# First group's loads reordered in a LoRA + dense kernel: identity behind W's first halves, W's blocks ahead of x, the adapters' rows spread over more steps, the small product one tile later

## The reference, cut to what matters

```python
x = x + (x @ B0[id0].T) @ A0[id0].T            # rank 16, scaling 1
x = x + x @ W.T + b + 2.0 * (x @ As[id1]) @ Bs[id1]   # W 2048 x 2048, rank 16
```

## Time and profile before

| | us |
|---|---|
| median of 3 runs | 1398.6 |
| lowest and highest of them | 1396.78, 1398.95 |
| the profiled execution's own time | 1398.88 |
| its span, first to last instruction | 1396.9 |
| PE busy in the span | 1372.8 |
| DVE busy | 943.6 |
| ACT busy | 529.1 |
| POOL busy | 79.1 |
| bytes moved by DMA | 311.60 MB, mean 223 GB/s |
| granted TensorE clock, mean | 0.997 |

### The profile page before, as it was taken

One profiled execution on the slowest core, in us unless ns is written; L12 is line 12 of the kernel. 1 busy time (PEld: TensorE's weight loads), 2 busy tenths in 40 slices (PEclk: granted clock), 3 DMA queues, 4 the chain that ended last, 5 costly groups with the idle time before them and its releaser, 6 DMA issues.

```text
span 1396.9 us, 16200 instructions
## 1 busy us (share of the span) xinstructions
PE 1372.8 (98%) x6024; PEld 1128.8 (81%) x6024; DVE 943.6 (68%) x1049; ACT 529.1 (38%) x588; POOL 79.1 (6%) x163
## 2 busy tenths in 40 slices
PE   6899999999999999999999999999999999999999
PEld 5788877888888878888888888888888888888887
DVE  4677897777877887687765566665755566665662
ACT  3444444433334443343324453333233444333321
POOL 2012010001010000001001000000101000000000
PEclk9999999999999999999999999999999999999999
DMA  9789764778888987599895335455856343555642
GB/s 343 242 293 306 264 238 147 243 236 282 297 292 307 314 297 264 178 301 327 287 358 194 110 112 180 163 175 168 276 204 189 117 135 134 169 167 189 194 151 83
DMA packets 98591, 311.60 MB, mean 223 GB/s; under 512 B 13009, under 2 KB 14289, under 8 KB 98513
## 3 DMA queue, kind: packets, MB, share of 16 engines
q1 hardware_dynamic: 92736, 298.96, 63.1%
q0 software_dynamic: 5776, 11.61, 2.9%
HBM read 254.94 MB, written 55.57 MB: 222 GB/s over the span
## 4 chain that ended last, share of the span: by engine, by line
PE 91%; DVE 4%; DMA 2%; issue 1%; ACT 1%; SPq 1%; ACTq 0%; DVEq 0%
PE acc L590 27%; PE acc L591 27%; PE acc L592 27%; DMA w_two<-w 2%; PE acc L565 2%; PE down_ps L549 2%; PE down_ps L550 2%; PE image_ps L535 1%; PE image_ps L529 1%; PE image_ps L530 1%; DVE w_one L759 1%; DVE bg_lo L794 1%; DVE w_lo L767 1%; DVE x_lo L789 0%; ACT w_hi L627 0%
## 5 line engine op out<-in xcount | busy, mean ns | idle before, releaser
L590 PE MATMUL acc<-x_hi,w_hi 128*128 128x512 f32 x1792 | 702.1, 392 | 16.3 <-DVE x_lo L789 12.5
L591 PE MATMUL acc<-x_lo,w_hi 128*128 128x512 f32 x1792 | 699.5, 390 | 0.0
L592 PE MATMUL acc<-x_hi,w_lo 128*128 128x512 f32 x1792 | 699.1, 390 | 0.0
L627 ACT ACTIVATE w_hi<-w_one 128x1024 fp32r<-128x1024 f32 x223 | 235.9, 1058 | 541.1 <-PE acc L592 504.5
L767 DVE TENSOR_TENSOR w_lo<-w_one,w_hi 128x1024 fp32r<-128x1024 f32 x223 | 273.1, 1225 | 215.2 <-ACT w_hi L627 215.2
L590 PEld LDWEIGHTS acc<-x_hi,w_hi 128*128 128x128 f32 x1792 | 337.6, 188 | 89.0 <-issue 16.6
L591 PEld LDWEIGHTS acc<-x_lo,w_hi 128*128 128x128 f32 x1792 | 337.6, 188 | 71.7 <-issue 1.0
L592 PEld LDWEIGHTS acc<-x_hi,w_lo 128*128 128x128 f32 x1792 | 337.3, 188 | 71.2
L660 ACT ACTIVATE sums<-acc 128x512 f32<-128x512 f32 x96 | 57.1, 594 | 203.7 <-PE acc L592 188.1
L826 DVE SCALAR_TENSOR_TENSOR sums<-acc,bias_sb,sums 128x512 f32<-128x512 f32 x128 | 95.7, 747 | 22.0 <-PE acc L565 20.8
L759 DVE TENSOR_TENSOR w_one<-w_one,w_two 128x1024 f32<-128x1024 f32 x79 | 96.4, 1220 | 17.1 <-DMA w_two<-w 17.1
(11 more groups left out here) (61 smaller groups left out, 610.3 us busy)
## 6 DMA issues: line engine op xcount, KB each, us to landing
w_one<-w SPq DMA_DIRECT2D x143, 512.0 KB, 5.5
w_one<-w_sums SPq DMA_DIRECT2D x80, 512.0 KB, 3.7
w_two<-w SPq DMA_DIRECT2D x79, 512.0 KB, 7.4
x_stage<-x SPq DMA_DIRECT2D x64, 512.0 KB, 4.4
out<-sums SPq DMA_DIRECT2D x128, 256.0 KB, 4.6
w_sums<-w_one SPq DMA_DIRECT2D x40, 512.0 KB, 4.1
resident<-x SPq DMA_DIRECT2D x32, 512.0 KB, 8.6
bg_raw<-w_rows SPq DMA_DIRECT2D x32, 512.0 KB, 5.0
```

The lines of the kernel that those rows point to most:

```text
L590: pe.matmul(ps[:, :], w_hi[ws][:, c, :], hi, start=(c == 0), stop=False)
L591: pe.matmul(ps[:, :], w_hi[ws][:, c, :], lo, start=False, stop=False)
L592: mm = pe.matmul(ps[:, :], w_lo[ws][:, c, :], hi, start=False, stop=(c == H - 1))
L627: act.activation(w_hi[s % W_PARTS][:, :, :], w_one[s % W_ONES][:, :, :], ACT.Copy).then_inc(w_hi_ready, 1)
```

## The change

It touches only the first group. SP loads the identity as its third transfer (behind the first halves of W's first two blocks) into a corner of `sums`, and ACT copies it into `identity_sb`; POOL no longer loads it. SP loads chunk 0 of batch 0's x ahead of the loop and chunks 1, 2, 3 at steps 0, 2, 3 (behind that step's W loads); A1's eight loads go to steps 1, 2, 3 as 2, 3, 3. POOL's eight A0 loads wait until `w_two` of step 1 has landed. The splits of A0's rows move from the loops' step 2 to step 3, A1's copy from step 3 to step 4 and behind split_bg, the small product behind step 5, its mask to step 6. Sums and splits of x for product 1 are at (1, 3, 6, 7) and (5, 6, 7, 7). The image chunks in steps 4 to 16 are distributed 1, 2, 3, 2, 3, 3, 2, 3, 3, 2, 3, 3, 2. `across` is multiplied ahead of chunk 7, 6, 6, 4 of its eight.

```diff
--- before.py
+++ after.py
@@ -52,15 +52,26 @@
 X_SPLIT_AT = (2, 4, 7, 7)
+A_RESIDENT_AT = {0: 1, 2: 2, 3: 3}
+A1_LOAD_AT = ((1, (0, 1)), (2, (2, 3, 4)), (3, (5, 6, 7)))
 def split_at(p):
-    return X_SPLIT_AT if p > 1 else (4, 5, 7, 7)
+    return X_SPLIT_AT if p > 1 else (5, 6, 7, 7)
+def sum_at(p):
+    return X_SUM_AT if p > 1 else (1, 3, 6, 7)
 IMAGE = 32
+ACROSS_AT = (7, 6, 6, 4)
 def where(s):
@@ -82,7 +93,7 @@
         places = (0, 2, 4, 6)
         return [IMAGE + 16 * g + 4 * i + places.index(o)] if i < 4 and o in places else []
     if 4 <= s <= 16:
-        counts = (2, 3, 2, 3, 2, 3, 2, 3, 2, 3, 2, 3, 2)
+        counts = (1, 2, 3, 2, 3, 3, 2, 3, 3, 2, 3, 3, 2)
         first = sum(counts[:s - 4])
         return list(range(first, first + counts[s - 4]))
     if 19 <= s <= 22:
@@ -246,6 +257,7 @@
         mask_sb = sums[1][:, 0, 0:P]
+        identity_raw = sums[0][:, 0, 0:P]
         across = sums[1][:, H - 1, T - P:T]
         a1_cols = sums[1][:, CH - 1:H - 1, :].rearrange("p o t -> p (o t)")
@@ -260,6 +272,7 @@
         mask_loaded = sem("mask_loaded")
         b1_rows_loaded = sem("b1_rows_loaded")
         identity_loaded = sem("identity_loaded")
+        identity_ready = sem("identity_ready")
         a1_ready = sem("a1_ready")
         across_done = sem("across_done")
         across_ready = sem("across_ready")
@@ -408,13 +421,14 @@
                 for tile, (k, q) in zip((w_one[0], w_two[0]), W_BLOCKS[0]):
                     sp.dma_start(tile[:, half, :], w[H * q][:, H * k:H * (k + 1), :][:, half, :])\
                       .then_inc(first_loaded[h], DMA)
+                if h == 0:
+                    sp.dma_start(identity_raw, identity).then_inc(identity_loaded, DMA)
                 load_resident(0, 1, h)
             for r in (2, 3):
                 load_resident(0, 1, r)
             load_w(1)
             load_w(2)
-            for r in range(2):
-                load_resident(0, 0, r)
+            load_resident(0, 0, 0)
             for s in range(STEPS):
                 g, i, o = where(s)
                 p = PRODUCTS * g + i
@@ -423,12 +437,12 @@
                     load_x(p + 1, X_LOAD_AT.index(o))
                 if s + W_ONES < STEPS:
                     load_w(s + W_ONES)
-                if s == 0:
-                    for r in (2, 3):
-                        load_resident(0, 0, r)
+                if s in A_RESIDENT_AT:
+                    load_resident(0, 0, A_RESIDENT_AT[s])
+                if s == A1_LOAD_AT[0][0]:
                     sp.wait_ge(ids_loaded, 2 * DMA)
-                if s in (0, 1):
-                    for n in range(4 * s, 4 * s + 4):
+                for t, ns in A1_LOAD_AT:
+                    for n in ns if s == t else ():
                         sp.dma_start(a1_raw[:, n, :, :], adapter(n, a1).rearrange("u p c r -> (u p) c r"))\
                           .then_inc(a1_loaded, DMA)
                 if s == 3:
@@ -490,10 +504,10 @@
                 pool.wait_ge(image_ready, j + 1)
                 pool.dma_start(images[:, T * j:T * (j + 1)], image[:, :]).then_inc(image_stored, DMA)
-            pool.dma_start(identity_sb[:, :], identity).then_inc(identity_loaded, DMA)
             pool.dma_start(ids_sb[:, 0, :], ids0).then_inc(ids_loaded, DMA)
             pool.dma_start(ids_sb[:, 1, :], ids1).then_inc(ids_loaded, DMA)
             pool.wait_ge(ids_loaded, 2 * DMA)
+            pool.wait_ge(w_two_loaded[1], DMA)
             for n in range(NB):
                 pool.dma_start(a0_raw[:, n, :, :], adapter(0, n, a0_down).rearrange("u p c r -> (u p) c r"))\
                     .then_inc(a0_loaded, DMA)
@@ -523,6 +537,10 @@
                         pe.wait_ge(image_ready, j - 1)
                     if z == 0:
                         pe.wait_ge(a0_ready, 1)
+                    if k == ACROSS_AT[j]:
+                        pe.wait_ge(across_ready, 1)
+                        pe.wait_ge(b1_rows_loaded, NB * DMA * (j + 1))
+                        pe.matmul(ps[:, :], across, b1_rows[:, :], start=False, stop=False).then_inc(b1_rows_used, 1)
                     for u in range(2):
                         c = 2 * k + u
                         wa = [t[:, c, :, :].rearrange("p n r -> p (n r)") for t in (a0_hi, a0_lo)]
@@ -534,10 +552,6 @@
                             pe.matmul(part, wa[1], identity_sb[:, :], start=False, stop=False)
                         mm = pe.matmul(ps[:, :], wa[0], lo[:, u, :], start=False, stop=(c == C - 1))
                     mm.then_inc(bg_used, 1)
-                    if k == (4 if j else 6):
-                        pe.wait_ge(across_ready, 1)
-                        pe.wait_ge(b1_rows_loaded, NB * DMA * (j + 1))
-                        pe.matmul(ps[:, :], across, b1_rows[:, :], start=False, stop=False).then_inc(b1_rows_used, 1)
                     return
                 if k == 0:
                     pe.wait_ge(down_ready, turn(n) + 1)
@@ -603,14 +617,14 @@
                     if c == 6 and len(zs) > 2:
                         multiply_chunk(zs[2])
-            for s in range(5):
+            for s in range(6):
                 step(s)
             pe.wait_ge(a0_loaded, NB * DMA)
             pe.wait_ge(a1_ready, 1)
             for c in range(C):
                 mm = pe.matmul(down_ps[:, 0:P], a1_cols[:, P * c:P * (c + 1)], a0_raw[:, :, c, :], start=(c == 0), stop=(c == C - 1))
             mm.then_inc(across_done, 1)
-            for s in range(5, STEPS):
+            for s in range(6, STEPS):
                 step(s)
             add_rank(STEPS - 1)
@@ -702,6 +716,8 @@
                     act.wait_ge(rank_done, H * m)
                 act.activation(rank_w[:, :], rank_raw[:, :], ACT.Copy).then_inc(rank_hi_ready, 1)
+            act.wait_ge(identity_loaded, DMA)
+            act.activation(identity_sb[:, :], identity_raw, ACT.Copy).then_inc(identity_ready, 1)
             act.wait_ge(w_made, 1)
             act.activation(w_hi[0][:, 0:CH, :], w_one[0][:, 0:CH, :], ACT.Copy).then_inc(first_hi_ready, 1)
             split_x(0, 0)
@@ -719,14 +735,10 @@
                     split_w(s + 1)
                 if s >= 1 and where(s - 1)[1] == 1:
                     copy(s - 1)
-                if s == 2:
+                if s == 3:
                     act.wait_ge(a0_loaded, NB * DMA)
                     act.activation(a0_hi[:, :, :, :], a0_raw[:, :, :, :].rearrange("p n c r -> p c n r"), ACT.Copy)\
                        .then_inc(a0_hi_ready, 1)
-                if s == 3:
-                    act.wait_ge(a1_loaded, NB * DMA)
-                    act.activation(a1_cols.rearrange("p (c n r) -> p c n r", c=C, n=NB),
-                                   a1_raw[:, :, :, :].rearrange("p n c r -> p c n r"), ACT.Copy).then_inc(a1_ready, 1)
                 if o in split_at(p + 1)[:2] and p + 1 < PRODUCTS * GROUPS:
                     split_x(p + 1, split_at(p + 1).index(o))
                 if s - 1 in LAST:
@@ -736,6 +748,10 @@
                 if s:
                     for z in background(s + 1):
                         split_bg(z)
+                if s == 4:
+                    act.wait_ge(a1_loaded, NB * DMA)
+                    act.activation(a1_cols.rearrange("p (c n r) -> p c n r", c=C, n=NB),
+                                   a1_raw[:, :, :, :].rearrange("p n c r -> p c n r"), ACT.Copy).then_inc(a1_ready, 1)
                 if s - 1 in LAST:
                     split_rank_x(LAST[s - 1])
                 if (i, o) in RANK_SPLIT:
@@ -864,7 +880,7 @@
             sum_half(0)
             dve.wait_ge(first_summed, 1)
-            dve.wait_ge(identity_loaded, DMA)
+            dve.wait_ge(identity_ready, 1)
             dve.scalar_tensor_tensor(out=w_one[0][:, 0, :], in0=f32(identity_sb[:, :]), scalar=W_IDENTITY[0],
                                      in1=w_one[0][:, 0, :], op0=ALU.mult, op1=ALU.add).then_inc(w_made, 1)
             split_half(0)
@@ -886,8 +902,8 @@
                 if 1 <= s < STEPS - 1:
                     split_w(s + 1)
                 if p + 1 < PRODUCTS * GROUPS:
-                    if o in X_SUM_AT:
-                        sum_x(p + 1, X_SUM_AT.index(o))
+                    if o in sum_at(p + 1):
+                        sum_x(p + 1, sum_at(p + 1).index(o))
                     if o in split_at(p + 1)[:2]:
                         split_x(p + 1, split_at(p + 1).index(o))
                 if s - 1 in LAST:
@@ -898,13 +914,13 @@
                     make_w(s + 2)
                     for z in background(s + 1):
                         split_bg(z)
-                if s == 2:
+                if s == 3:
                     dve.wait_ge(a0_hi_ready, 1)
                     dve.tensor_tensor(a0_lo[:, :, :, :], a0_raw[:, :, :, :].rearrange("p n c r -> p c n r"),
                                       f32(a0_hi[:, :, :, :]), ALU.subtract).then_inc(a0_ready, 1)
                 if s >= 1:
                     complete(s - 1)
-                if s == 5:
+                if s == 6:
```

## The result

| | before | after |
|---|---|---|
| median of 10 runs each, same chip | 1397.96 | 1402.57 |
| lowest and highest of them | 1396.73, 1400.62 | 1400.82, 1405.14 |
| the profiled execution's own time | 1398.88 | 1401.94 |
| its span | 1396.9 | 1399.9 |

The ratio is 1.0033, with a 95% interval of 1.0025 to 1.0041: the change makes the kernel 4.6 us slower (3.5 to 5.7). The forecast was 1396.2 with a range up to 1402.0.

A forecast was written before the change was run, and what follows sets the result against it. PE is busy 98% of the span, so only its idle and slow time, early on, can be won. 1398.9 - 0.4 - 7.1 + 2.25 + 2.4 + 0.4 = 1396.4, or 1396.2 against the median; range 1393.5 to 1402.0.

The forecast's parts named there:

- Part 3: New PE stall at step 4's first image chunk, from DVE's order of operations: 2.25 us, bounds 1.1 and 5.4.
- A0's rows come late: Rival: POOL's eighth load waits again, rows land at 37.3, chunk 0 stalls 5.4 us, clock lost: 1402.3, chance 0.13.
- The rival's sum: Total for late A0 rows: 1396.2 + 3.2 + 2.9 = 1402.3 us.
- Start of step 1: Step 1 begins 0.4 us earlier, range -0.6 to +0.5.
- Before step 4: PE's 2.84 us wait for W's block goes; 3.0 us counted from PE's starts, part of the 7.1 removed.
- The clock: A stall that loses the granted clock costs 2.9 us, taken from the earlier slow stretch: (6.8 - 1.0) / 2.
- Step 8: New PE stall at tile 4: three chunks there make x's chunk 2 late, 2.4 us, bounds 0 and 2.9.
- no stall in step 8: Rival: x's chunk 2 is in time after all, so step 8 hardly stalls: 1393.8, chance 0.15.
- Step 10: Step 9, also with three chunks, leaves DVE 0.4 us late at step 10.
- The question whether POOL's loads queue behind SP's backlog: Claimed they don't: SP's loads of W took 8.4 us, POOL's 5.4 in the same stretch.
- the main forecast of 1396.2: Whole kernel with both new stalls and the clock kept: 1396.2, own range 1395.0 to 1397.6, chance 0.42.

The follow-up runs named there:

- the edit on the kernel before: The kernel before with the chunk counts of steps 7 to 10 as 2, 3, 3, 2 instead of 3, 2, 3, 2: 1401.09 against 1398.41, ratio 1.0025.
- its removal: The changed kernel with the chunk counts of steps 7 to 10 as 3, 2, 3, 2 instead of 2, 3, 3, 2: median 1400.64, ratio 1.0019.
- the sixteen matmuls: The changed kernel with sixteen matmuls into a spare bank, whose output nobody reads, ahead of chunk 0: median 1402.48, ratio 1.0034.

## Why the prediction was wrong

**The step that failed** is Part 3's stall at chunk 0, 2.25 us with the clock kept: it took A0's rows and the chunk's own operand as there in time. The trace has 5.69 us by starts (5.54 idle) and 1.7 us of slow clock on top, for both were late. What let the first of them pass is in the rival "A0's rows come late": "The identity's load was then ahead of them in POOL's queue and is now gone, which speaks for the wait to come behind the eighth", and with it the chance of 0.13. The wait belongs to the count of 128-row loads, and came behind seven loads of A0's rows in all sixteen profiled kernels with a scratch size of 1024, with 5.16 to 5.83 us. The identity's load, which had landed before the first of them, had not counted: with it and without it the wait stayed ahead of the same load. A row that I had read, 5.27 us ended by nothing in the profile, was explained away instead of carried along: with the loads moved 7 us later (10.38 to 17.45), the wait moves with them, from 18 to 23.3 us, where PE has time to spare, to 25 to 30.6, where it has none. The earlier trace rows gave no reason for the wait to move to another load.

**The rival's sum** was 1402.3 against a measured 1402.57, and the late rows are what ended last at chunk 0. That the totals meet is in part luck: the rival's sum is 3.7 us above its base of 1398.6, while the medians of ten runs are 4.6 us apart and the profiled pair 3.06. Term by term, in the profiled pair:

- Start of step 1: forecast -0.4, the trace has -0.9. Later kernels with the same loads up to there started step 1 anywhere from 19.23 to 20.62, so neither number is resolved by one execution. The identity's addition was at 5.93 (forecast 6.4), and PE's start was still set by the second halves, summed at 9.49, as the working said.
- Before step 4: forecast -3.0, measured -3.0. The block of step 4 was summed at 28.55 (forecast landing 29).
- Chunk 0: the rival's 5.4 us, measured 5.69 by starts. Part 3's own working, DVE's order, holds: 2.28 by starts where PE came late enough for everything else, and 1.14 us idle with the sum moved and all loads in time. (the earlier trace rows show the copy behind step 4, not step 5, made late because ACT waited for a chunk; the 1.56 us from it to w_lo, which the working uses, come again from 80.48 to 82.04.)
- The clock: 2.9 us forecast, 1.7 us in the profile. The 2.9 us had been taken from a stretch in which PE worked nearly throughout. Here the slow stretch began inside the idle one, and cost only what was left of it.
- Step 8: forecast +2.4. The ledger has +2.46, the edit on the kernel before +2.7, its removal -1.9. The case "no stall in step 8", with 0.15, was wrong.
- Step 10: forecast 0.4. The trace has a wait of 0.37 us there, and the ledger shows +1.03 over steps 9 to 19. PE's starts place most of the other 0.7 us. Where `across` is multiplied in step 15, 0.68 us lie between the matmul ahead of its product and the one behind it (159.18 to 159.86). In step 10 it is 1.31 us (below), 0.37 of it the wait, and in step 13 0.95 us (136.17 to 137.12), for an operand that DVE finished only just in time. That makes 0.9 of the 1.03.

```profile
106.43 0.39 PE L606 MATMUL acc<-x_hi,w_lo 128*128 128x512 f32 x1
107.18 1.12 PE L543 MATMUL image_ps<-b_rows,sums 128*128 128x512 f32 x2 [0.37 <-DVE bg_lo L810]
107.74 0.79 PE L547 MATMUL image_ps<-bg_hi,a_hi 128*128 128x512 f32 x1
```

By the ledger that is -0.9 - 3.0 + 3.3 + 2.5 + 1.2 = +3.1 us, the profiled pair's 3.06, where the rival's terms make +3.6. Its total came close because errors of both signs are in it: the clock too dear by 1.2 us and step 1's gain too small by 0.5, the late operands of steps 10 and 13 left out.

**What was missing altogether** is the second cause. Part 3 took chunk 0's operand as there in time. Its load stood behind A1's on SP, and once A0's rows were early it was the one that PE waited for, with a scratch size of 2048 as with the eighth load on SP. Had the eighth load not waited, the kernel would have lost 3.9 to 4.8 us at chunk 0 all the same (3.89, 4.81, 4.78 in three profiles), and the main forecast of 1396.2 would still have failed. The trace of the kernel before had a row for this too, which the prediction doesn't read: ACT waiting for chunk 0's load, at 40.97.

```profile
40.97 1.06 ACT L671 ACTIVATE bg_hi<-bg_raw 128x1024 fp32r<-128x1024 f32 x1 [1.26 <-DMA bg_raw<-w_rows]
```

The question whether POOL's loads queue behind SP's backlog was answered as forecast: POOL's first seven took 5.3 to 5.8 us from issue to landing after the change (5.4 in the earlier trace rows), while SP's load of chunk 0, four times as large, took 7.1, and 10 in the kernel with the chunk loads first.

**What stays open:** how much of the 4.6 us in the medians is the clock (1.4 to 1.7 us in profiles, not resolved in medians); where the 1.5 us lie by which the medians are further apart than the profiled pair; why the chunk's load gained 3.9 us from 0.75 MB less; and whether a scratch size of 2048 pays in a kernel that keeps its three slots.

## What to carry to other kernels

A load that is moved later takes its queue's own waits along (5.27 us before, 5.61 after), and an idle time whose cause the profile doesn't name has to be moved with it until it is explained. When a stall has several feeders (here A0's rows, the chunk's own load, and DVE's order), taking away one shows the next at almost the same time: work out each feeder's arrival, not just the one that is named, and judge edits together, since the same move was worth nothing on one kernel and some 2 us on another. What a queue has been given ahead of a load counts as well as the load's place: with 0.75 MB less ahead it landed at 33.2 and came in time; issued 2 to 4 us sooner, but with those bytes ahead, it had landed at 36.9 and 37.1.

## What the runs showed of the hardware that I had not expected

- With `dynamic_dma_scratch_size=1024` POOL issues seven loads of 128 rows one behind another, idle for 0.58 to 0.76 us between them; the eighth load, of 128 rows or of B's 16, is issued 0.39 us behind the seventh's landing: idle for 5.16 to 5.83 us in sixteen profiles. A load that had landed before the first of the seven (the identity's, at 8.3 in the kernel before, against 10.38) did not count. With 2048 POOL is idle for 0.62 us ahead of the eighth, as ahead of the others (one profile).
- Behind the start, the granted clock fell to 0.50 at every idle time of PE of 2.84 us and more, for 3.4 or 6.8 us each time, twelve in as many profiles (2.84 to 5.54 us). At 2.1 us both happened: it held in two profiles (2.12 us without POOL's wait, 2.11 with the sixteen matmuls) and fell in two (2.12 us without POOL's wait and with two chunks in step 8, 0.66 in the window 45 to 50; 2.08 us in the kernel before with three chunks in step 8, 0.73 in that window, not long after an idle time of 2.06 us behind which it had held). It held behind 2.25 us in step 8 in all seven profiles that have it, behind 2.48 us in one (at 142.15, scratch size 2048), and behind 1.77 us and less (0.95 us in the kernel before: 1.00 from 20 to 30 us). So a clock lost to the forecast's stall of 2.25 us was never seen at that length, but just below it was, and one profile doesn't say how often.
- Two kernels with the same instructions up to step 1 (the eighth load on SP and two chunks in step 8, without and with the later sum) start PE's first matmul at 12.11 and at 10.82 us, so a gain of half a microsecond at the start can't be read from one pair of profiles.
